# Moving POOL's look-ups and DVE's compares inside a node step, building the source matrix from a key row in memory, and taking edge totals from the scaled matrix

## What is computed

```python
x = ln(x + sage(x, edges))          # layer 0: mean over in-edges @ W_l.T + b + x @ W_r.T, twice, relu between
x = ln(x + propagate(x, edges, 10)) # layer 1: see below
x = ln(x + attention_ffn(x, edges)) # layer 2: 8 heads over in-edges, layernorm, FFN of width 32, layernorm
x = ln(x + tensor_product(x, edges))# layer 3: irreps 128 + 3 x 128, gates, edge messages, linear maps

# layer 1
sim  = exp(cos(x[row], x[col]) / (4 * exp(sigma)**2)),  0 inside the exp where row == col
sup  = edge_weight * sim
norm = segment_sum(sup, row)
for _ in range(10):
    out = (x * b + (segment_sum(sup * out[col], row) + out) * a) / (b + norm * a + a)
```

## Time and profile before

| | us |
|---|---|
| three timed executions | 2785.2, 2775.96, 2782.85 |
| median | 2782.85 |
| the profiled execution, device time | 2781.79 |
| its span in the trace | 2780.0 |
| PE busy | 2290.1 (82%) |
| DVE busy | 1806.6 (65%) |
| POOL busy | 1135.8 (41%) |
| ACT busy | 1008.9 (36%) |
| mean granted clock of TensorE | 0.898 |

### The profile page before, as it was taken

One profiled execution on the slowest core, in us unless ns is written; L12 is line 12 of the kernel. 1 busy time (PEld: TensorE's weight loads), 2 busy tenths in 40 slices (PEclk: granted clock), 3 DMA queues, 4 the chain that ended last, 5 costly groups with the idle time before them and its releaser, 6 DMA issues.

```text
span 2780.0 us, 28864 instructions
## 1 busy us (share of the span) xinstructions
PE 2290.1 (82%) x9582; PEld 1197.5 (43%) x9582; DVE 1806.6 (65%) x3856; ACT 1008.9 (36%) x1735; POOL 1135.8 (41%) x869
## 2 busy tenths in 40 slices
PE   8999999999999689996076766739998898389786
PEld 4455555555555345453031211214444553254465
DVE  7999888888878861445753433544567658557753
ACT  2354545454555432210432322321121132265553
POOL 2766654455675724301645665620210201233222
PEclk9999999999999889998587988869999697599898
DMA  7333443333343435325744645670210202222221
GB/s 245 99 103 105 118 121 120 104 118 108 108 111 104 129 95 167 104 76 165 206 139 134 175 131 155 153 222 10 67 48 27 73 1 74 75 71 69 57 57 53
DMA packets 214547, 298.62 MB, mean 107 GB/s; under 512 B 100006, under 2 KB 100501, under 8 KB 213018
## 3 DMA queue, kind: packets, MB, share of 16 engines
q1 hardware_dynamic: 108186, 213.98, 25.7%
q0 software_dynamic: 106240, 83.12, 12.1%
HBM read 171.66 MB, written 160.65 MB: 120 GB/s over the span
## 4 chain that ended last, share of the span: by engine, by line
PE 56%; DVE 20%; issue 7%; POOL 6%; DMA 5%; ACT 5%; SPq 1%; POOLq 0%; DVEq 0%; ACTq 0%
PE bank L2031 8%; PE bank L320 8%; PE bank L1010 7%; PE bank L304 5%; POOL arena L1624 4%; PE bank L2627 3%; PE bank L296 3%; PE bank L990 2%; PE bank L311 2%; DMA arena<-y_table,ids 2%; DVE st L642 2%; POOL arena L1102 2%; PE bank L312 2%; PE bank L2510 2%; DMA x_table<-arena 2%
## 5 line engine op out<-in xcount | busy, mean ns | idle before, releaser
L1102 POOL DMA_INDIRECT arena<-x_table,idd x120 | 152.0, 1267 | 648.2 <-DVE arena L2297 157.1
L1678 PE MATMUL bank<-arena 125*125 125x512 f32 x360 | 207.5, 709 | 108.6 <-DMA arena<-y_table,ids 103.7
L2031 PE MATMUL bank<-arena 128*125 128x512 f32 x640 | 293.7, 614 | 1.4 <-DVE Md L2251 0.7
L304 PE MATMUL bank<-arena 128*125 128x512 f32 x640 | 285.2, 599 | 8.6 <-DMA ident<-ident_in 8.6
L1624 POOL DMA_INDIRECT arena<-y_table,ids x180 | 229.6, 1276 | 153.1 <-DMA y_table<-arena 101.0
L320 PE MATMUL bank<-arena 128*125 128x512 f32 x640 | 278.5, 593 | 2.1 <-ACT arena L517 1.8
L1852 DVE SCALAR_TENSOR_TENSOR arena<-arena,v,bank 125x512 f32<-125x512 f32 x180 | 134.3, 746 | 188.1 <-PE bank L1678 180.0
L811 POOL TENSOR_TENSOR arena<-arena,rowv 125x512 f32<-125x512 f32 x80 | 99.5, 1278 | 315.4 <-DVE arena L725 201.7
L1018 ACT ACTIVATE arena<-bank 128x500 f32<-128x500 f32 (+1 forms) x210 | 114.6, 589 | 279.3 <-PE bank L962 145.4
L1010 PE MATMUL bank<-arena 128*125 128x512 f32 x480 | 208.8, 593 | 0.0
L1729 ACT ACTIVATE bank<-arena 125x512 f32<-125x512 f32 x180 | 107.6, 600 | 267.5 <-DVE arena L1852 262.4
(11 more groups left out here) (404 smaller groups left out, 4417.4 us busy)
## 6 DMA issues: line engine op xcount, KB each, us to landing
y_table<-arena SPq DMA_DIRECT2D x36, 896.0 KB
p_table<-arena SPq DMA_DIRECT2D x25, 896.0 KB
z_table<-arena SPq DMA_DIRECT2D x25, 896.0 KB
x_table<-arena SPq DMA_DIRECT2D x25, 896.0 KB
arena<-x_cols SPq DMA_DIRECT2D x20, 1000.0 KB, 6.4
arena<-x SPq DMA_DIRECT2D x20, 896.0 KB
out<-arena SPq DMA_DIRECT2D x20, 896.0 KB
x_by_src<-arena SPq DMA_DIRECT2D x5, 896.0 KB
```

What stands on the lines that cost most here:

```text
L304: i = nc.tensor.matmul(b[0:P, :], xT[:, k, j * P:(j + 1) * P], W1r[:, k, :], start=k == 0, stop=k == KC - 1)
L1102: nc.gpsimd.indirect_dma_start(out=dst, out_offset=None, in_=table, in_offset=bass.IndirectOffsetOnAxis(ap=idx, axis=0), bounds_check=limi ...
L1678: nc.tensor.matmul(bank[t % RING1][0:P, :], Ss[:, t, :], V1[:, t, :], start=False, stop=True, skip_group_check=True).then_inc(P_sum, 1)
L2031: i = nc.tensor.matmul(b[0:P, :], fT[:, k, j * P:(j + 1) * P], W[:, k, :], start=k == 0, stop=k == KC - 1)
```

## The change

1. No hardware loop: LOOP_START and LOOP_END are both 12, and all 24 steps are written out.
2. The compares of list q=1 move from place 1 of steps 2 to 7 to places 2 and 3 of steps 2 to 11: in `z_tiles`, ahead of the third and the fourth tile (`in_gap`).
3. The look-ups and the scatters move from behind all of POOL's step to right behind the additions L798, ahead of stage B's work. The scatters are in steps 13 to 16. `dve_records` runs in step 12 in three parts: ahead of `z_tiles`, and in the two gaps. `sp_records` moves to step 11; the loads back stay at step 17 and DVE's reading at 18.
4. The source matrix: behind the stores of p, SP copies the column of source keys of the sorted records within memory into a row, `src_row`; behind job z4 of layer 0 it loads that row into all 125 partitions of `Ss` (1.25 MB). DVE copies the first and last key of each tile and compares in place over 125x2500. `diag1`, its product, the ten matmuls and the compares from banks are gone, and POOL no longer waits for them.
5. The barrier behind layer 0 and its counter are gone (the diff removes `end_phase` and all its calls). POOL and SP still wait for the stores of z and x1 that end layer 0.
6. Layer 1's scalars: the mask of row == col is taken before the waits for ACT, the reciprocal waits for the root alone, not for the exponentials.
7. The totals are products of the **scaled** `Ss` with ones, group by group (`group_totals`, in banks 4 and 6 by turns), each ahead of its group's own products; `ratio` is taken per group. DVE scales group 0 first, then `BM`, then groups 1 to 4, without waiting for totals.

Addresses and counts follow (SEG at 3780, `rec_back` to 16 * 9).

```diff
-        LOOP_START, LOOP_END = 8, NG - 6
-        COUNTED = {(1, 0): (0, 1, 14), (1, 1): (0, 14, ET), (2, 1): (1, 1, 8), (3, 1): (1, 8, 11), (4, 1): (1, 11, 14),
-                   (5, 1): (1, 14, 16), (6, 1): (1, 16, 18), (7, 1): (1, 18, ET)}
+        LOOP_START = LOOP_END = NG - 8
+        COUNTED = {(1, 0): (0, 1, 14), (1, 1): (0, 14, ET), (2, 2): (1, 1, 4), (2, 3): (1, 4, 7), (3, 2): (1, 7, 8),
+                   (3, 3): (1, 8, 10), (4, 2): (1, 10, 11), (4, 3): (1, 11, 12), (5, 2): (1, 12, 13), (5, 3): (1, 13, 14)}
+        COUNTED.update({(t - 8, 3): (1, t, t + 1) for t in range(14, ET)})
...
+            def in_gap(place):
+                count_pass(place)
+                if isinstance(s, int) and s == LOOP_END:
+                    dve_records(dve, c, place)
+
             def z_tiles(part, j0):
                 for q in range(2):
                     j = j0 + q
+                    if j0:
+                        in_gap(j)
...
+            if isinstance(s, int) and 1 <= s <= 7:
+                pool_look_up(pool, 6 * s - 6, min(6 * s, 2 * ET))
+            if isinstance(s, int) and s in RECORDS:
+                pool_records(pool, *RECORDS[s])
...
+        def dve_records(dve, c, part):
+            less_d, eq_d, less_s, eq_s = (found[:, :, :, k] for k in range(4))
+            if part == 0:
+                dve_record_ranks(dve, c, less_d, eq_d, less_s, eq_s)
+            elif part == 2:
+                dve_record_sources(dve, c, less_d, less_s)
+            elif part == 3:
+                dve_record_columns(dve, c, less_s)
...
+        def dve_source_matrix(dve, c, q, key, S):
+
+            nc.vector.tensor_copy(ck[:, q, 0:ET], S[:, :, 0])
+            link(dve, c, nc.vector.tensor_copy(ck[:, q, ET:NB], S[:, :, P - 1]))
+            nc.vector.tensor_tensor(S, S, b3(key, P), ALU.is_equal)
             link(dve, c, nc.vector.tensor_tensor(many[:, q, :], ck[:, q, 0:ET], ck[:, q, ET:NB], ALU.not_equal))
...
-        RECORDS = {LOOP_END + k: (10 * k, 10 * k + 10) for k in range(4)}
+        RECORDS = {LOOP_END + 1 + k: (10 * k, 10 * k + 10) for k in range(4)}
...
+            with nc.allow_non_contiguous_dma(reason="the source keys of sorted records as a row"):
+                sp.dma_start(src_row[0], RSd[:, Q_SRC]).then_inc(rec_back, 16)
             sp.wait_ge(T_sb, jobs0_moved("z", 3))
             sp.dma_start(W2l, w_l2).then_inc(w0_in, 16)
             sp_ext(sp, V0x, BF0, 2)
+            sp.wait_ge(R_sb, jobs0_done("z", EG - 1))
+            sp.wait_ge(rec_back, 16 * 7)
+            sp.dma_start(Ss, src_row[0].rearrange("(t f) -> t f", f=P).partition_broadcast(P)).then_inc(rec_back, 16)
...
-            pool.wait_ge(R_sb, c.r + EG)
...
+            def group_totals(g):
+                pe.wait_ge(w1_rdy, g + 1)
+                if g >= 2:
+                    pe.wait_ge(P_raw, TG * (g - 1))
+                for j in range(TG):
+                    q = nc.tensor.matmul(totals[g][:, j:j + 1], Ss[:, TG * g + j, :], ones[:, 0:1], start=j == 0,
+                                         stop=True, skip_group_check=True)
+                q.then_inc(totals_rdy, 1)
...
+                group_totals(g)
...
-            dve_build(dve, c, 1, RSs[:, :, 1], Ss, None, diag1)
+            dve.wait_ge(rec_back, 16 * 8)
+            dve_source_matrix(dve, c, 1, RSs[:, :, 1], Ss)
...
+            link(dve, c, nc.vector.tensor_tensor(TMP, RSs[:, :, 0], RSs[:, :, 1], ALU.not_equal))
+            link(dve, c, nc.vector.tensor_tensor(SD, SD, TMP, ALU.mult))
+            sg = v20[:, 8, 0:1]
+            dve.wait_ge(sc1a, 1)
             link(dve, c, nc.vector.reciprocal(v20[:, 5:7, :], v20[:, 5:7, :]))
             link(dve, c, nc.vector.tensor_tensor(SD, SD, SSQ, ALU.mult))
             link(dve, c, nc.vector.tensor_tensor(SD, SD, DSQ, ALU.mult))
-            link(dve, c, nc.vector.tensor_tensor(TMP, RSs[:, :, 0], RSs[:, :, 1], ALU.not_equal))
-            link(dve, c, nc.vector.tensor_tensor(SD, SD, TMP, ALU.mult))
-            sg = v20[:, 8, 0:1]
+            dve.wait_ge(sc1a, 2)
             link(dve, c, nc.vector.tensor_tensor(sg, abv[:, 2:3], abv[:, 2:3], ALU.mult))
             link(dve, c, nc.vector.tensor_scalar_mul(sg, sg, 4.0))
             link(dve, c, nc.vector.reciprocal(sg, sg))
             nc.vector.tensor_scalar(SD, SD, sg, None, ALU.mult).then_inc(sc1, 1)
             dve.wait_ge(sc1a, 3)
             al, be, both = abv[:, 0:1], abv[:, 1:2], v20[:, 9, 0:1]
-            nc.vector.tensor_tensor(both, al, be, ALU.add)
-            nc.vector.tensor_tensor(SUP, SD, RSs[:, :, 2], ALU.mult).then_inc(sc1, 1)
-            dve.wait_ge(sc1, 3)
+            link(dve, c, nc.vector.tensor_tensor(SUP, SD, RSs[:, :, 2], ALU.mult))
+
+            def scaled(g):
+                Sg = Ss[:, g * TG:(g + 1) * TG, :]
+                nc.vector.tensor_tensor(Sg, Sg, b3(gcols(SUP, g), P), ALU.mult).then_inc(w1_rdy, 1)
+            scaled(0)
             nc.vector.tensor_tensor(BM[:, :, 0:NM], BM[:, :, 0:NM], b3(SUP, NM), ALU.mult).then_inc(bm_rdy, 1)
-            for g in range(EG):
-                Sg = Ss[:, g * TG:(g + 1) * TG, :]
-                dve.wait_ge(totals_rdy, TOT0 + g + 1)
-                nc.vector.tensor_tensor(Sg, Sg, b3(gcols(SUP, g), P), ALU.mult).then_inc(w1_rdy, 1)
+            link(dve, c, nc.vector.tensor_tensor(both, al, be, ALU.add))
+            for g in range(1, EG):
+                scaled(g)
 
             def ratio(rr, minus, total, n):
                 nc.vector.tensor_scalar_mul(minus, total, -1.0)
...
-            ratio(RR, NRR, totals, P)
             for t in range(ET):
+                if t % TG == 0:
+                    dve.wait_ge(totals_rdy, TOT0 + t // TG + 1)
+                    ratio(gcols(RR, t // TG), gcols(NRR, t // TG), totals[t // TG], P)
...
-            end_phase(pe, c)
```

More of the change, by code:

```diff
@@ L208, in node_steps @@
                 k = st_.end
-            lo, hi = LOOP_START // 2, LOOP_END // 2
-            with eng.Fori(lo, hi) as i:
-                kk = k
-                for par in range(2):
-                    st_ = Step(i * 2 + par, kk)
-                    st_.shift = {"t": i * (2 * FULL_T) - 2 * FULL_T * lo, "r": i * (2 * FULL_R) - 2 * FULL_R * lo}
-                    step(st_, i * 2 + par, par)
-                    kk = st_.end
-            n = hi - lo
-            k = {"t": k["t"] + 2 * FULL_T * n, "r": k["r"] + 2 * FULL_R * n}
             for s in range(LOOP_END, STEPS):
@@ L1210, in dve_records_back, with dve_build @@
             link(dve, c, nc.vector.tensor_scalar_add(bkm[:, :, :], bkm[:, :, :], -1.0))
-        def dve_build(dve, c, q, key, S, M, dg):
+        def dve_build(dve, c, q, key, S, M):
             dve.wait_ge(dstep, c.d)
-            if dg is not None:
-                nc.vector.tensor_tensor(dg[:, :, :], spread(ident[0:P, 0:P], ET), b3(key, P),
-                                        ALU.mult).then_inc(s_end, 1)
             for g in range(EG):
@@ L1225, in dve_build @@
                 nc.vector.tensor_copy(gcols(ck[:, q, 0:ET], g), row[:, :, 0])
-                i = nc.vector.tensor_copy(gcols(ck[:, q, ET:NB], g), row[:, :, P - 1])
-                if M is None:
-                    i.then_inc(R_sb, 1)
-                    continue
+                nc.vector.tensor_copy(gcols(ck[:, q, ET:NB], g), row[:, :, P - 1])
                 nc.vector.tensor_tensor(M[:, g * TG:(g + 1) * TG, :],
@@ L1233, in dve_build @@
             dve.wait_ge(R_sb, c.r)
+            link(dve, c, nc.vector.tensor_tensor(many[:, q, :], ck[:, q, 0:ET], ck[:, q, ET:NB], ALU.not_equal))
+        def dve_source_matrix(dve, c, q, key, S):
+            nc.vector.tensor_copy(ck[:, q, 0:ET], S[:, :, 0])
+            link(dve, c, nc.vector.tensor_copy(ck[:, q, ET:NB], S[:, :, P - 1]))
+            nc.vector.tensor_tensor(S, S, b3(key, P), ALU.is_equal)
             link(dve, c, nc.vector.tensor_tensor(many[:, q, :], ck[:, q, 0:ET], ck[:, q, ET:NB], ALU.not_equal))
@@ L1575, in gnn_kernel @@
         Y1_0 = 2 * TG * EG
-        totals = bank[4][0:P, 0:ET]
-        totals_rdy, TOT0 = s_end, 2
+        totals = [bank[4 + 2 * (g % 2)][0:P, TG * g:TG * (g + 1)] for g in range(EG)]
+        totals_rdy, TOT0 = s_end, 1
         BM = at(2500, [ET, 32], P)
@@ L1647, in first_own @@
                                  stop=True).then_inc(P_sum, 1)
-            pe.wait_ge(sc1, 3)
-            for t in range(ET):
-                q = nc.tensor.matmul(totals[:, t:t + 1], Ss[:, t, :], SUP[:, t:t + 1], start=t == 0, stop=True,
-                                     skip_group_check=True)
-                if t % TG == TG - 1:
-                    q.then_inc(totals_rdy, 1)
+            def group_totals(g):
[6 more added lines that the diff above has]
+                q.then_inc(totals_rdy, 1)
             for g in range(EG):
                 tiles = range(TG * g, TG * (g + 1))
+                group_totals(g)
                 for t in tiles[:-1]:
@@ L2941, in step @@
```

(2 more changed lines are left out.)

43 lines of the change are left out of this document (11 added, 32 removed).

## The result

| | median us | lowest to highest | runs |
|---|---|---|---|
| kernel before | 2784.02 | 2775.96 to 2792.22 | 6 |
| changed kernel | 2757.57 | 2749.69 to 2765.92 | 6 |

The ratio is 0.9906 with a 95% interval of 0.9883 to 0.9929: 26 us faster, by the interval 20 to 33. The profiled executions agree: a span of 2753.4 us against 2780.0, 26.6 less. The forecast was 2750, 32 us faster, in a range of 2740 to 2768.

A forecast was written before the change was run, and what follows sets the result against it. TensorE's pace was taken as the floor, with other engines holding it up above that. Node part -19.8 and layer 1 -12.3 sum to -32.1: from 2781.8 to 2749.7, forecast as 2750 us, range 2740 to 2768.

The forecast's parts named there:

- Look-ups (-15.3): Node loop, steps 4 to 8: look-ups behind POOL's additions bring the steps to 45.41 us each, 15.3 us back.
- First steps (-1.0): Steps 1 and 2: earlier additions no longer hold a 125x4 tensor_scalar of 1.71 us; -1.0 us, ends 0 and -1.7.
- Compares (0): Node loop: key compares fit DVE's waits ahead of the third and fourth z tiles; 0 us, end +0.8.
- the first rival: Gap before the fourth z tile: POOL's additions hold compares, 2.2 us in each of eight steps; 2767 us, chance 0.06.
- Records (5.3 left, -3.9): Records' steps: 9.2 us above the floor falls to 5.3 on TensorE's path; -3.9 us, ends -6.3 and 0.
- Written-out steps (+0.4): Steps 8 to 13 without hardware loop: 45.48 against 45.41 us, six steps at 0.07, +0.4 us.
- Source matrix (first part of -9.5): Layer 1's start, without build and barrier: last gather issued 7.5 us sooner, 2.0 less landing backlog; -9.5 us.
- the second rival: Layer 1: gathers bound by data, squares only 6.1 us earlier, totals' order worth nothing; 2755 us, chance 0.17.
- Scalars (-1.3): Layer 1: first five scalar operations run inside the wait for ACT's exponentials; -1.3 us, ends -0.9 and -1.3.
- totals (-1.5): Layer 1: totals per group let the first product start about 6.2 us earlier; net -1.5, ends +0.7 and -2.7.
- The copy (0): Behind the last store of p: copying 2500 keys keeps SP 5.6 us, no cost with 62 us to spare.

The follow-up runs named there:

- e4: Kernel before with one edit: look-ups of steps 1 to 7 right behind the additions to x's rows; median 2768.12 us, ratio 0.9935.
- e3: Changed kernel with look-ups and scatters back at the end of POOL's step; median 2776.43 us, ratio to the kernel before 0.9963.
- e8: Changed kernel with the compares of list 1 directly ahead of the first z tile in steps 2 to 11, not in the gaps; 2758.86 us.
- e11: Kernel of e1 with all three parts of the records' arithmetic early in step 12; median 2754.84 us, ratio 0.9855.
- e1: Changed kernel with the copy of the 2500 keys issued behind the fourth store of p instead of the last; median 2749.56 us, ratio 0.9862.
- e10: Kernel of e1 with the first two parts of the records' arithmetic early in step 12, the third left in the gap; median 2750.04 us, ratio 0.9876.
- e12: Changed kernel with the records of e11 and the copy of the keys moved behind V0x's loads; median 2747.31 us, ratio 0.9876.
- e2: Changed kernel with the copy of the keys issued twice in a row, the second into a row nobody reads; 2767.23 us.

## Why the forecast held, and where it failed

- **Look-ups (-15.3)**: right in mechanism and size, -15.0. One move makes it (e4), undoing it takes it back (e3).
- **First steps (-1.0)**: not confirmed. The hold that I named is gone (1.71 us before, 0.17 now), and step 2 took 38.47 us instead of 39.54. But at the end of step 2 a tensor_scalar of the same shape now waits 5.15 us beside the additions, and step 1 scatters: the changed kernel had +0.7 in all, and the stretch takes 109.9 to 113.6 us among the kernels. Timeline of DVE and POOL, changed kernel:

```profile
121.44 5.15 DVE L759 TENSOR_SCALAR dd<-mv 125x4 f32<-125x4 f32 x1
121.64 4.92 POOL L796 TENSOR_TENSOR arena<-arena,rowv 125x512 f32<-125x512 f32 x4
```

- **Compares (0)**: right, and the first rival is out: 2.68 us beside POOL. That their place doesn't matter either way (e8) I hadn't said.
- **Records (5.3 left, -3.9)**: 4.0 left. The size was right, the reason half: I counted the ten us as work to be covered, while about half of it was POOL's hold on small operations (10.0 us against 4.8 with POOL idle). Moved to where POOL is idle the same operations cost 0.7 (e11).
- **Written-out steps (+0.4)**: 45.48 against 45.41, as said.
- **Source matrix (first part of -9.5)**: the compare's 2.8 and the 7.5 at the last issue were right (2.76 and 7.6); the first gather starts 0.9 behind the landing, not 0.3. The step that failed is that the landing would gain 2.0 more: the engines were full at the end as before (landing 11.27 us), so the scalars came only 6.9 sooner here, and 6.2 in the mean of the executions with and without the edit. That is the second rival's -6.1, which had 0.17; its other half, that the totals' order would give nothing, didn't come.
- **Scalars (-1.3) and totals (-1.5)**: -0.9 and -2.5: the scalars at the low end given, the totals near the good end, since the later totals ran at the upper clock.
- **The copy (0)**: this is the step that was wrong. I priced it at 5.6 us, the time a transfer of 2500 rows holds SP, and asked only who stands behind it on SP's queue, with 62 us to spare. SP let go after 1.42 us. The cost was on the DMA engines, which the last store of p and the gathers of its rows needed next: 8.0 us in the profiled execution, 6.8 to 8.0 in six. The change's diff could have told it: the new transfer stands directly behind the store that releases those gathers.
- **What made up for it**: 4.9 us in the stretch up to the last store of p. The kernel with only look-ups moved had 257.8 there too and five kernels with the change's code 262.6 to 262.9, so nothing ties it to the change. This is luck, of the two executions that were profiled: without it the profiled gain would have read 22 us. The medians don't rest on these two, but their interval, 20 to 33 us, holds 22 as well as 27. By medians the kernel took 7.6 us more than the forecast 2750, the size of the copy's cost, and with the copy moved and nothing else (e1) the median was 2749.56.

The Trainium skill (DMA: Bandwidth & Descriptors, Rules for kernel authors) has a non-contiguous last dimension as one descriptor per element. The runs agree: the page of the profile counts 100006 packets under 512 B in the kernel before, 102521 with one copy of 2500 elements and 105031 with two, and the copy of 10 KB took 14.5 us by itself.

## What to carry to other kernels

Price a transfer three times: for its issue on the queue, for its landing, and for the time it takes from the DMA engines when others need them; put one of many small elements where nobody waits for the engines, not behind a store that someone waits for. On POOL, let additions whose data come early stand first, and put short transfers that nobody waits for behind them, in front of work that has to wait anyway: the additions then start early and don't fall on DVE's critical operations. Small DVE operations belong where POOL is idle: beside its additions each takes 1.2 us instead of 0.2.

## What the runs showed of the hardware

- POOL's additions hold DVE in two ways. One DVE operation waited for a whole run of four (squares 7.32 us, an addition 6.02 us that had begun 0.5 us ahead of them, e3; a tensor_scalar of 125x4 4.76 us); the records' operations of 125x20 got in one per addition, 1.2 us each, beside L820 and L797 alike (e10). What decides between the two stays open. Copies and tensor_scalars with one operand were held as well (1.2 to 1.3 us each, e10), the compare with accumulator was not (2.68 us for 125x2375).
- A gather right behind the barrier took 3.00 to 3.32 us on POOL in four executions, the same one without the barrier 1.42 to 1.56 in ten.
- 2500 elements of 4 bytes, memory to memory: 14.5 us with otherwise idle engines, 5.8 ns each (e12). SP was held for 0.74 to 1.49 us by one such copy, and for 6.85 us by a second one right behind it (e2).
